# Second layer of a two-layer kernel: where the router, the rank computation and one sequence's projections stand

## The reference

```python
def reference(...):                      # x: (4, 512, 128) float32
    x = L0_attn(layernorm(x)) + ...      # windowed attention and a 16-expert MLP: not touched by the change
    # second layer, on h = layernorm(x):
    qkv = h @ w_qkv                      # 16 heads of 8
    att = softmax(q @ k.T / sqrt(128)) @ v
    a   = att @ w_out
    score = relu(h @ rw1 + rb1) @ rw2 + rb2         # 128 -> 512 -> 8 experts, for each of 2048 rows
    gate  = softmax(score restricted to its two largest)
    m   = sum over experts of gate[e] * (relu(h @ W1[e] + b1[e]) @ W2[e] + b2[e])
    return x + a + m
```

## Time and profile before

| | us |
|---|---|
| median of three runs | 1305.83 (1301.24 to 1307.26) |
| the profiled execution, own time | 1307.18 |
| its span, first to last instruction | 1305.5 |
| second layer, setup block | 799.3 to 862.7 |
| stage 0 (front of sequence 0) | 863 to 928.3 |
| stage 1 (front 1, back 0) | 928.3 to 1031.5 |
| stages 2, 3 | 1031.5 to 1234.9 |
| stage 4 (back 3, gathering, end) | 1234.9 to 1305.5 |

### The profile page before, as it was taken

How to read it: one execution, slowest core, us unless ns; L and a number is a source line. 1 busy time by engine, 2 the same in 40 slices (tenths; PEclk the granted TensorE clock), 3 DMA queues, 4 the chain that set the end, 5 groups by cost and what they waited for, 6 DMA issues and landing times. The chain is left out here.

```text
span 1305.5 us, 23034 instructions
## 1 busy us (share of the span) xinstructions
PE 1050.9 (81%) x9629; PEld 542.6 (42%) x9629; DVE 980.7 (75%) x1266; ACT 816.8 (63%) x857; POOL 140.1 (11%) x208
## 2 busy tenths in 40 slices
PE   2589999889759599999987588656679989989787
PEld 1333333333448133333333577232234655546232
DVE  6699999999714999999997535259448567666746
ACT  1689999999623699999996521310156455564354
POOL 3000000000400100000001202306200000000630
PEclk9889999999869699999999687875679899998788
DMA  7300000000191200000000860002113423431110
GB/s 260 100 8 2 1 2 1 2 1 1 63 197 32 49 1 2 1 2 1 2 1 1 170 121 21 1 0 91 38 33 113 130 82 98 129 89 50 47 35 25
DMA packets 74822, 65.29 MB, mean 50 GB/s; under 512 B 6660, under 2 KB 67552, under 8 KB 74720
## 3 DMA queue, kind: packets, MB, share of 16 engines
q1 hardware_dynamic: 72672, 59.64, 18.4%
q0 software_dynamic: 2048, 4.20, 1.1%
HBM read 39.70 MB, written 20.97 MB: 46 GB/s over the span
## 5 line engine op out<-in xcount | busy, mean ns | idle before, releaser
L538 DVE SCALAR_TENSOR_TENSOR ring<-AD,PT 128x1808 f32<-128x1808 f32 (+15 forms) x128 | 284.3, 2221 | 5.1 <-POOLq L520 3.2
L683 PE MATMUL LG<-ring,lred 128*32 128x456 f32 (+15 forms) x2048 | 233.3, 575 | 1.3 <-ACT ring L635 1.3
L1609 ACT ACTIVATE EX<-SS 128x1024 f32<-128x1024 f32 x128 | 130.9, 1028 | 105.3 <-PE SS L1480 104.3
L1698 DVE TENSOR_REDUCE MX<-SS 128x2 f32<-128x1024 f32 x128 | 152.9, 1213 | 52.9 <-PE SS L1480 52.4
L625 ACT ACTIVATE ring<-ring 128x3616 f32<-128x3616 f32 (+15 forms) x50 | 169.9, 3398 | 3.7 <-DVE ring L538 3.7
L705 PE MATMUL SD<-DS,eyes 96*32 96x456 bf16 (+15 forms) x2496 | 156.0, 369 | 9.8 <-ACT ring L630 7.7
L633 ACT ACTIVATE ring<-ring 128x1824 f32<-128x1824 f32 (+15 forms) x78 | 141.0, 1807 | 0.0
L705 PEld LDWEIGHTS SD<-DS,eyes 96*32 96x32 bf16 x2496 | 57.7, 96 | 153.4 <-ACT ring L630 56.5
L1480 PE MATMUL SS<-KS,QS 32*128 32x512 f32 x256 | 75.2, 584 | 51.1 <-DVE MX L1698 46.0
L538 DVE SCALAR_TENSOR_TENSOR ring<-AD,bdmg 128x1808 f32<-128x1808 f32 (+15 forms) x50 | 110.7, 2214 | 0.0
L718 PE MATMUL PY<-w2T,xg 128*128 128x128 f32 x512 | 74.1, 288 | 35.3 <-DVE xg L563 35.3
(11 more groups left out here) (300 smaller groups left out, 1493.6 us busy)
## 6 DMA issues: line engine op xcount, KB each, us to landing
wide<-band SPq DMA_DIRECT2D x64, 158.0 KB, 10.9
w1s<-in_L_ffn_W SPq DMA_DIRECT2D x39, 256.0 KB, 3.0
w2s<-in_L_ffn_W SPq DMA_DIRECT2D x39, 256.0 KB, 3.0
band<-zs SPq DMA_DIRECT2D x8, 1024.0 KB, 9.0
band<-Z SPq DMA_DIRECT2D x4, 1024.0 KB, 8.5
xs<-Z SPq DMA_DIRECT2D x4, 640.0 KB, 8.2
xl<-xs SPq DMA_DIRECT2D x10, 256.0 KB, 2.9
ys<-yo SPq DMA_DIRECT2D x10, 256.0 KB, 3.0
```

The costliest lines, as they stand in the source:

```text
L538: return v.scalar_tensor_tensor(out=ring[:, slot, s, :, t0:T], in0=AD[:, s, :, j + t0:j + T], scalar=extra, in1=AD[:, s, :, PAD + t0:PAD + T],
L683: mm = pe.matmul(LG[32 * b:32 * b + 32, par, s, t0:T], lred[:, s, n % 4, :], ring[:, slot, s, b, t0:T], start=(n % 4 == 0), stop=(n % 4 == 3))
L1609: act.activation(EX[:, Q % 2, hh:hh + 2, t, :], SS[:, slot, :, :], ACT.Exp, scale=SCALE1).then_inc(freed[slot], 1)
L1698: v.tensor_reduce(MX[:, t, p // 2, hh:hh + 2], SS[:, slot, :, :], AX.X, ALU.max).then_inc(freed[slot], 1)
```

## The change

1. The router leaves the setup block and runs within stage 0, after the front's task of a step: hidden products 0 to 7 two at a time at steps 0 to 3 and 8 to 15 one at a time at steps 4 to 11, scores at 12, the transposition at 13, `top_experts` on VectorE at 14, the counts at 16, the gates' transpositions at 18 to 21, the bias products at 22 to 25, and their additions on VectorE (`add_bias`) at 24 to 27. Its large buffers (`HR`, `rw1`, ...) now lie in `EX`, which is not in use before stage 1; its products go to the experts' two PSUM banks `PHh`, to `PN` and to `PYy`.
2. `dispatch` runs on GpSimd. It reads the counts from SBUF, where ScalarE copies them. Reductions become additions of halves, and a fused compare becomes two instructions: 54 instructions and an iota in place of 41.
3. The tasks q0, q1, k0, k1 and v of sequence 1 move from stage 1 to stage 0, at steps 24, 27, 30, 33 and 36. Stage 0 has 44 steps (39 before) and stage 1 has 35 (39 before), so the list of pieces puts 25 into stage 1 (29 before), and 27 into stage 3 (23 before).
4. The 24 copies of the q and k weights go from GpSimd to ScalarE, six before each of its copies of `xT`; GpSimd's clearing of `VA` and `NX` goes to the start of the main block, and its small constants go between the reciprocal roots (`powers`).

```diff
+MOVED_AT = 24
...
+    EX = sb("EX", [P, 2, 4, NT, T], F32, l1)
+    spare = EX[:].rearrange("p a h t k -> p (a h t k)")
+    HR = spare[:, 0:8192].rearrange("p (a b t) -> p a b t", a=FQ, b=B)
...
         def _(act):
+            def copies(q):
+                for dst, n in ((wq, 0), (wk, 1)):
+                    for s in range(3):
+                        act.copy(dst[:, q, :, s, :], wqkv[:, n, 32 * q:32 * q + 32].rearrange("p (h d) -> p h d", d=HD))
+
+            act.wait_ge(w_ready, 1)
+            act.wait_ge(d_w[0], 16 * 7)
             for b in range(B):
+                copies(b)
                 act.wait_ge(xT_pe, b + 1)
                 act.copy(xT[:, b, :], S[b][:, :]).then_inc(xT_sb, 1)
...
+    moved = [x for x in fronts[1] if x[1][0] in "qkv"]
+    fronts[1] = [x for x in fronts[1] if x not in moved]
+    for n, x in enumerate(moved):
+        fronts[0].insert(MOVED_AT + 3 * n, x)
...
+    HIDDEN_STEPS, SCORE_STEP, TURN_STEP, TOP_STEP, COUNT_STEP, GATE_STEP, BIAS_STEP = 8, 12, 13, 14, 16, 18, 22
+
+    def units_of(n):
+
+        if n < 4:
+            return range(2 * n, 2 * n + 2)
+        return range(n + 4, n + 5) if n < 4 + HIDDEN_STEPS else range(0)
...
     def _(pool):
...
-        pool.wait_ge(slots_ready, 1)
+        pool.memset(VA[:], 0.0).then_inc(ms_ready, 1)
...
+        pool.memset(NX[:], 0.0).then_inc(ms_ready, 1)
+        link = chain_of(pool, s_disp)
+
+        def dispatch():
+            pool.wait_ge(gate_ready, 1)
...
+            pool.wait_ge(counts_sb, 1)
+            src, step = tot, 1
+            for n in range(4):
+                dst = cum[:, n % 2]
+                pool.tensor_copy(dst[:, 0:step, :], src[:, 0:step, :])
+                link(pool.tensor_tensor(dst[:, step:, :], src[:, step:, :], src[:, :TT - step, :], ALU.add))
+                src, step = dst, 2 * step
...
+            for k in range(K1):
+                link(pool.tensor_scalar(pick1[:, 1], pick1[:, 0], float(k + 1), 1.0, ALU.is_equal, ALU.mult))
+                link(pool.tensor_tensor(pick1[:, 1], pick1[:, 1], gt[:], ALU.mult))
+                pool.tensor_tensor(cum[:, 0], pick1[:, 1], rank[:], ALU.mult)
+                link(pool.tensor_tensor(cum[:, 1], pick1[:, 1], gate[:], ALU.mult))
+                for w in (4, 2):
+                    link(pool.tensor_tensor(cum[:, :, :, 0:w], cum[:, :, :, 0:w], cum[:, :, :, w:2 * w], ALU.add))
+                pool.tensor_tensor(slotf[:, k, :], cum[:, 0, :, 0], cum[:, 0, :, 1], ALU.add)
+                link(pool.tensor_tensor(gates[:, k, :], cum[:, 1, :, 0], cum[:, 1, :, 1], ALU.add))
+            link(pool.tensor_copy(sloti[:], slotf[:]))
+
+        dispatch()
...
+        def router_hidden(i):
+            a, b = i % 4, i // 4
+            if i >= 2:
+                pe.wait_ge(hr_sb, i - 1)
+            pe.matmul(PHh[:, i % 2].rearrange("p n t -> p (n t)"), rw1[:, P * a:P * a + P], xT[:, b, :], start=True, stop=True
+                      ).then_inc(hr_pe, 1)
...
+        def count():
+            pe.wait_ge(gate_ready, 1)
...
+        def bias_out(i):
+            pe.wait_ge(gt_sb, 4)
+            if i >= 2:
+                pe.wait_ge(b2_sb, i - 1)
+            for n in range(4):
+                last = pe.matmul(PHh[:, i % 2, n, :], gateT[:, 4 * i + n, :], b2r1[:], start=True, stop=True)
+            last.then_inc(b2_pe, 1)
...
     @block.scalar
...
+        def route(n):
+            for i in units_of(n):
+                act.wait_ge(hr_pe, i + 1)
+                act.activation(HR[:, i % 4, i // 4, :], PHh[:, i % 2].rearrange("p n t -> p (n t)"), ACT.Relu, bias=rb1c[:, i % 4:i % 4 + 1]
+                               ).then_inc(hr_sb, 1)
+            if n == SCORE_STEP:
+                act.wait_ge(sc_pe, 1)
+                act.copy(scT, PN[:]).then_inc(sT_sb, 1)
...
     @block.vector
...
-                    if s == 0 and name == "k1":
-                        dispatch()
+                if s == 0 and n == TOP_STEP:
+                    top_experts()
+                if s == 0 and BIAS_STEP + 2 <= n < BIAS_STEP + 6:
+                    add_bias(n - BIAS_STEP - 2)
```

More of the change, by code:

```diff
@@ L1093, in _, with powers @@
             link(pool.affine_select(out=low[:], in_=ones[:], compare_op=ALU.is_gt, fill=0.0, base=0, pattern=[[1, P]], channel_multiplier=-1))
-            for b in range(B):
+            def powers(b):
                 r = slice(NT * b, NT * b + NT)
@@ L1126, in _ @@
             pool.memset(zcol[:], 0.0)
[L1127 to L1132, removed]
+            powers(3)
         @block.vector
@@ L1253, in second_layer @@
     HB = sb("HB", [P, 2, FQ, P], F32, l1)
+    unused = HB[:].rearrange("p n a t -> p (n a t)")
+    counts = unused[:, 0:2 * P].rearrange("p (n t e) -> p n t e", n=2, t=TT)
+    below, twice = unused[:, 2 * P:2 * P + TT], unused[:, 2 * P + TT:2 * P + TT + E1]
     w1s = sb("w1s", [P, AHEAD, FF], F32, l1)
@@ L1530, in project_last @@
                     mm.then_inc(last_out, 1)
-        pe.wait_ge(ms_ready, 2)
-        counted = gt[:].rearrange("p t e -> p (t e)")
-        pe.matmul(PHh[:, 0, 0, :], low[:], counted, start=True, stop=True)
-        pe.matmul(PHh[:, 1, 0, :], ones[:], counted, start=True, stop=True).then_inc(counts_pe, 1)
+        def router_hidden(i):
[4 more added lines that the diff above has]
+                      ).then_inc(hr_pe, 1)
@@ new lines, in router_scores, with router_turn @@
+        def router_scores():
+            pe.wait_ge(hr_sb, 16)
+            for a in range(FQ):
+                for b in range(B):
+                    last = pe.matmul(PN[32 * b:32 * b + 32, :], rw2[:, a, :], HR[:, a, b, :], start=(a == 0), stop=(a == FQ - 1))
+            last.then_inc(sc_pe, 1)
+        def router_turn():
+            pe.wait_ge(sT_sb, 1)
+            for n in range(NT):
+                last = pe.transpose(PYy[:, n, :], scT[:, P * n:P * n + P], ident[:])
+            last.then_inc(sT_pe, 1)
@@ new lines, in count, with gate_turn @@
+        def count():
+            pe.wait_ge(gate_ready, 1)
+            counted = gt[:].rearrange("p t e -> p (t e)")
+            pe.matmul(PN[:, 0:P], low[:], counted, start=True, stop=True)
+            pe.matmul(PN[:, P:2 * P], ones[:], counted, start=True, stop=True).then_inc(counts_pe, 1)
+        def gate_turn(i):
+            if i >= 2:
+                pe.wait_ge(gt_sb, i - 1)
+            for n in range(4):
+                last = pe.transpose(PHh[0:E1, i % 2, n, :], gate[:, 4 * i + n, :], ident[:])
+            last.then_inc(gt_pe, 1)
@@ new lines, in bias_out @@
+        def bias_out(i):
+            pe.wait_ge(gt_sb, 4)
+            if i >= 2:
+                pe.wait_ge(b2_sb, i - 1)
+            for n in range(4):
+                last = pe.matmul(PHh[:, i % 2, n, :], gateT[:, 4 * i + n, :], b2r1[:], start=True, stop=True)
+            last.then_inc(b2_pe, 1)
+        def route(n):
+            for i in units_of(n):
+                router_hidden(i)
+            if n == SCORE_STEP:
+                router_scores()
+            if n == TURN_STEP:
+                router_turn()
+            if n == COUNT_STEP:
+                count()
+            if GATE_STEP <= n < GATE_STEP + 4:
+                gate_turn(n - GATE_STEP)
+            if BIAS_STEP <= n < BIAS_STEP + 4:
+                bias_out(n - BIAS_STEP)
@@ L1686, in low_part @@
+        link = chain_of(v, s_dve)
         def low_part(b, name):
```

216 lines of the change are left out of this document (90 added, 126 removed).

## The result

The changed kernel takes 1296.18 us (median of 14 executions, 1286.46 to 1302.38) where the kernel before, on the same chip, takes 1306.55 (1301.24 to 1314.6): ratio 0.9905, 95% interval 0.9884 to 0.9927. It is faster, by 0.95%; the forecast said 2.1%, and 1296 lies above its range of 1267 to 1292. The profiled execution took 1301.07, with a span of 1299.3. The 14 executions go with the granted clock (1286.46 at a mean of 0.895, 1301.15 at 0.882; correlation -0.90), so the one that was profiled lies near the slow end: against it the forecast's 1279.6 is 21.5 us short, against the median 18.

What follows compares the result with a forecast made beforehand. No one engine was taken to bound the whole second layer; VectorE was the bound in stage 0. 1307.2 - 44.7 + 39.8 - 24.2 + 1.5 = 1279.6, the median 1.35 under the profiled execution: 1278 us, range 1267 to 1292.

Steps and rivals of the forecast that it cites:

- Setup: Setup block before q0: router gone, clearing moved, q0 starts at 819.3 where it was 863.97; -44.7 us, 4.7 from the clearing.
- (a): Stage 0, steps 0 to 3: hidden products and relus delay k1's low part to 19.2 us after q0's start; +7.6.
- (b): Stage 0: dispatch leaves VectorE; -9.1 us.
- (d): Stage 0: top-k on VectorE, bare since VectorE is the bound; +6.5 us.
- (e): Stage 0, steps 15 to 23: gates' and bias groups lengthen TensorE's step beyond the maxima's 1.13 us; +3.2 us.
- (c): Stage 0, steps 4 to 14: score tile and hidden product exceed the maxima, and router scores delay the next tile; +5.2 us.
- rival 2: TensorE stays at 1.2 GHz in stage 0's steps 4 to 25: +12 us, 1290; chance 0.10.
- (f): Stage 0, steps 24 to 41: additions 2.8, bias products 2 x 1.9, four moved projections 18.0, v 1.8; +26.4 us.
- Stages 2 to 4: Stage 3 takes four pieces at steps with slack, +1.5 us; nothing for stages 2 and 4, the later gather being covered.
- Late tiles (1): Dispatch lasts 28 to 43 us and stage 1's first piece waits up to 15: 1279 to 1293; chance 0.12.
- a slow dispatch (4): GpSimd's dispatch so slow that late tiles eat all; no gain left at 56 us; chance 0.07.
- Rival 3: Stage 1 is bound by TensorE and takes 90 us in place of 79: 1289; chance 0.05.

Runs made afterwards that it cites:

- e9: The kernel before with only GpSimd's clearing of NX and VA (and the waits for it) moved to the main block: 1337.21 us, 0.9973 of the kernel before.
- e3: The changed kernel with four useless TensorE products after step 3 of stage 0, during the wait for k1: 1329.71 us, 0.9903 of the kernel before.
- e4: The changed kernel with ScalarE doing the front's high part before the router's relus in a step: 1323.68 us, 0.985 of the kernel before.
- e5: The changed kernel with VectorE's bias additions one step earlier and ahead of the front's task: 1328.95 us, 0.9893 of the kernel before.
- g2: g1 with the change's move of sequence 1's projections and v (steps 24 to 36) put back: 1282.79 us.
- g1: e6 with plain DMAs to and from fixed rows in place of the 32 scatters and 32 gathers, leaving out row routing: 1277.36 us.
- e2: The changed kernel with dispatch back on VectorE, in its old 41 instructions, after step 17 of stage 0: 1347.13 us, 1.0013 of the kernel before.
- g3: g1 with q0, q1, k0, k1 of sequence 1 moved to steps 11, 12, 15 and 16 of stage 0, v left in stage 1: 1265.69 us.
- e6: The changed kernel without the move of sequence 1's projections, ScalarE's front task first and bias additions first: 1308.33 us, 0.9723 of the kernel before.
- a0: The changed kernel, unaltered, as the yardstick beside the experiments: 1334.07 us, 0.9913 of the kernel before.
- f4: e6 with q0, q1, k0, k1 of sequence 1 moved to steps 11, 12, 15 and 16 of stage 0: 1315.42 us, 0.9776 of the kernel before.
- b0: The kernel before, unaltered, run for a profile on the chip of a0: 1342.24 us, a single execution.

## Why the prediction was wrong

**Setup: right.** -43.7 for -44.7 us. The clearing's 4.7 us came as forecast (1.11 for 5.82, and e9 for it alone). The Trainium skill (SBUF — State Buffer, § Who interferes with whom) has the lock taken by tensor_scalar in a two-port mode and not by a reduction; the trace agrees with both halves: 5.82 beside the clearing and 1.11 without it, and the maxima beside GpSimd's dispatch stay at 1.22 to 1.23. Which mode the tensor_scalar ran in, no run here shows.

**Stage 0, (a), (b), (d), (e): right.** 19.8 for 19.2 us in (a), dispatch off VectorE in (b), 6.5 for top-k in (d), 13.4 for 13.4 in (e).

**Stage 0, (c): the first step that failed.** "1.37 against 1.13 for the maxima (...): 8 x 0.24 = 1.9" prices TensorE at 2.4 GHz for all of steps 4 to 11. The stretch took 25.4 us for the 18.3 forecast (10 maxima at 1.13, v's 1.8, and 5.2). Of the 7.1 that it took more, 5.6 are the slow steps (857.01 - 841.00 = 16.0 for seven steps, at 1.485 each 10.4) and 0.8 that a fast step is 1.485 and not 1.37; 0.7 is left over. That is rival 2 for the first half of its stretch, and it came from a wait that the prediction itself had built in: ScalarE's two relus before k1's high part, in (a), leave TensorE nothing to do for 3.15 us. The prediction had named a TensorE at 1.2 GHz in steps 4 to 11 as a sign of being wrong, but had not asked what its own (a) would do to TensorE. e3 and e4, which fill or shorten that wait, have no slow step.

**Stage 0, (f): the term mis-sized.** 45.2 for 41.1 us (13 maxima at 1.13, and 26.4). The moved projections, "4.0 to 4.85 net, four of them 18.0", took 21.0: 15.9 of idle time before the four low parts (5.33, 3.00, 3.89 and 3.71) and 5.1 of low parts. The bias products, 2 x 1.9, took 4.9, which e5 takes away by order alone.

**Stages 2 to 4: the second step that failed.** "Stage 3 takes the four pieces, at steps that had slack: +1.5" and nothing for stages 2 and 4. The three stages took 8.6 us more. Stages 2 and 3 of the kernel before, busy time by stretch (here from q0 to q0):

```profile
1031.50:1133.00 101.50, 94.18 (x607) 56.34 (x607) 68.31 (x69) 58.21 (x109) 0.00 (x0) 0.97 0.36 102
1133.00:1234.90 101.90, 87.52 (x515) 47.77 (x513) 67.96 (x70) 51.53 (x86) 16.62 (x17) 0.90 0.25 69
```

Stage 2 was TensorE's already, 94.2 us busy of 101.5. With the boundaries of the table it was 94.5 for 611 matmuls, and with the list of pieces shifted it became 95.6 for 620. Stage 3's busy time rose in the same way from 87.7 to 93.1 us (517 matmuls to 545), and 4.5 of those 5.4 came through: it had no slack to speak of. Stage 4 has the same 298 matmuls, but TensorE was busy for 60.9 us in place of 59.0, at a granted clock of 0.78 in place of 0.81, and it took 1.6 us longer. g2 against g1 shows the same three differences with nothing changed but the move: 2.5, 4.4 and 1.4. That the added matmuls cause those of stages 2 and 3, and the clock that of stage 4, is read from these rows and was not tested by itself.

**Stage 1: right in kind.** -22.7 for -24.2.

**The move in sum.** The forecast's own terms for it are +18.0 and +1.8 in stage 0, -24.2 and +1.5: a gain of 2.9. g1 and g2 give +22.3, -23.0, +8.3: a loss of 7.6. So half of the error of 21 us is the move, a part of the change that works against it.

**The rivals.** Late tiles (1) and a slow dispatch (4) fell: 21.2 us for the 21 taken, well under 28. The Trainium skill (GPSIMD Engine Reference, § Performance versus the Vector engine) gave 22 by its two-input figure, an estimate, and the trace agrees; a two-input operation on 128x128 took 0.45 us on GpSimd and 0.28 to 0.29 on VectorE (e2), 1.6 times; no run has one of 2048 elements. Rival 3, a stage 1 bound by TensorE, fell (70.0 busy of 80.0), but its mechanism sat in stage 2, where I had not looked. Rival 2 came half true: TensorE was at 1.2 GHz for steps 4 to 8 (0.50), at 2.4 for steps 9 to 12 (1.00), and at 1.2 again from step 15 on (0.50 from 872.0 to 885.4), where (e) had priced the score tile at 0.8 us, its time at that level.

Between the two profiles the span fell by 6.2 us (10.4 by the medians, where 28 were forecast): setup -43.7 and stage 1 -22.7 against stage 0 +51.6 and stages 2 to 4 +8.6.

Open: how the placement of g3 does with real scatters where there are no stand-stills (by g3 some 8 to 12 us under e6; it was not run there), and what the engines wait for in the stand-stills.

## What to carry to other kernels

Work that is moved off a serial stretch should go where the bound engine already waits, not where it is busy: four projections cost 4.3 us in the router's wait and beside top-k, and 22 (with v) among the maxima, in the runs with plain DMAs. Price the handing over between engines as well as their busy time, and when work moves between stages, look at every stage that the rest of a list then shifts into. Within a step, give the shared engine's first turn to the task that the others wait for: that order alone (e4) was worth more here than dummy matmuls that keep TensorE's clock up.

## What the runs showed of the hardware

In every profile of the runs a0 to f4 ScalarE, VectorE and TensorE stand still for some 3 to 15 us at a time while GpSimd runs its indirect DMAs, and the trace names no releaser in the program ("remote" or "issue"); of VectorE's in stage 0 the longest is 14.88 us, in e2. Part of these times can be one engine waiting for another that stands still. The kernel before, ScalarE in stage 4, in b0:

```profile
1257.21 1.02 ACT L1609 ACTIVATE EX<-SS 128x1024 f32<-128x1024 f32 x1 [8.71 <-issue]
1270.62 1.02 ACT L1609 ACTIVATE EX<-SS 128x1024 f32<-128x1024 f32 x1 [12.39 <-issue]
1279.09 2.93 ACT L1609 ACTIVATE EX<-SS 128x1024 f32<-128x1024 f32 x3 [7.45 <-remote]
```

and the same line on the first chip:

```profile
1254.43 1.02 ACT L1609 ACTIVATE EX<-SS 128x1024 f32<-128x1024 f32 x1 [1.51 <-PE SS L1480]
1256.16 1.02 ACT L1609 ACTIVATE EX<-SS 128x1024 f32<-128x1024 f32 x1 [0.70 <-PE SS L1480]
```

Stage 0 (with the scatters) is 82.8 us in b0 for 64.3, and stage 4 (with the gathers) 84.9 for 70.5: 33 of the 35 us between the two spans (1340.5 and 1305.5). With plain DMAs (g1) the stand-stills are gone. The same kernel took 2.8 to 3.0% longer beside the experiments, on four chips, than beside the result. Whether that belongs to the chips or to something else in which the sets differ (what ran beside them, for instance) is not shown. So a stretch with indirect DMAs should be compared within one set on one chip only.

TensorE's level after a stand-still is not the same in every execution. After the same 3.14 or 3.15 us of idle time a0 ran its first two score tiles at 0.50 us and was at 1.2 GHz by the third, while the profile after began at 0.79:

```profile
834.29 0.50 PE L1500 MATMUL SS<-KS,QS 32*128 32x512 f32 x2 [3.14 <-DVE KS L1741]
...
838.21 0.79 PE L1500 MATMUL SS<-KS,QS 32*128 32x512 f32 x2
```

With 0.85 us of idle time (e4) it didn't fall. Work does not bring the level back at once: in the profile after TensorE had no gap from 840.17 to 853.0 and stayed at 0.50 all that time, and from 872.0 to 885.4 it was busy for 13.1 of 13.4 us at 0.50 and did not rise at all. So a short wait of 3.15 us was followed by 13 us at half the clock.
